# A macaron block on one core: the down product of an FFN chunk stands four chunks behind its gate product instead of three, and its input has five buffers instead of four

## The reference

```python
x = x + 0.5 * ffn(layernorm(x))
x = x + attn(layernorm(x))
x = x + 0.5 * ffn(layernorm(x))
```

```python
scores = sigmoid(x @ gate_w); topk_w, topk_i = top_k(scores, 6)
combine = sum(one_hot(topk_i) * (topk_w / sum(topk_w)))
act = silu(x @ wg) * (x @ wu)                 # all 32 experts
routed = einsum('tef,efd,te->td', act, wd, combine)
shared = silu(x @ sg) * (x @ su) @ sd
```

## Time and profile before

| | |
|---|---|
| median of 3 runs | 1780.58 us (1778.83 to 1783.36) |
| the profiled execution, its own time | 1783.27 us |
| its span, first to last instruction | 1781.4 us |
| mean granted TensorE clock | 0.958 of full speed |
| busy share PE / DVE / POOL / ACT | 87% / 71% / 56% / 47% |

### The profile page before, as it was taken

One profiled execution on the slowest core, in us unless ns is written; L12 is line 12 of the kernel. 1 busy time (PEld: TensorE's weight loads), 2 busy tenths in 40 slices (PEclk: granted clock), 3 DMA queues, 4 the chain that ended last, 5 costly groups with the idle time before them and its releaser, 6 DMA issues. The chain is left out here.

```text
span 1781.4 us, 22496 instructions
## 1 busy us (share of the span) xinstructions
PE 1551.8 (87%) x7088; PEld 1165.3 (65%) x7088; DVE 1265.5 (71%) x2067; ACT 843.5 (47%) x1692; POOL 988.8 (56%) x1048
## 2 busy tenths in 40 slices
PE   5998887887899889888998799879987998889979
PEld 4665554546566567666776677667765776667868
DVE  4553587876868788968797879778977787777321
ACT  4443454543555346535553466346634564444323
POOL 1663354654767457636665566447644666458525
PEclk9999999999999999999999999999998999889989
DMA  4565221123323232423232333233322333233434
GB/s 161 205 217 192 75 95 50 63 77 103 133 90 113 97 121 92 138 88 116 95 126 96 98 115 128 89 104 116 126 95 73 124 114 113 80 112 131 133 100 149
DMA packets 73430, 202.35 MB, mean 114 GB/s; under 512 B 10049, under 2 KB 22561, under 8 KB 72929
## 3 DMA queue, kind: packets, MB, share of 16 engines
q1 hardware_dynamic: 65120, 175.75, 29.6%
q0 software_dynamic: 8192, 25.17, 4.6%
HBM read 175.46 MB, written 25.43 MB: 113 GB/s over the span
## 5 line engine op out<-in xcount | busy, mean ns | idle before, releaser
L1478 POOL TENSOR_TENSOR ring<-ring 128x512 f32<-128x512 f32 x192 | 256.9, 1338 | 378.9 <-DVE ring L1358 378.6
L808 PE MATMUL gub<-x_hi,wr 128*128 128x384 f32 (+2 forms) x1040 | 428.9, 412 | 29.1 <-DVE hid L1175 22.4
L889 PE MATMUL acc<-hid,w_down 128*128 128x384 f32 (+2 forms) x1040 | 408.1, 516 | 15.6 <-POOL hid L1457 15.5
L1457 POOL TENSOR_TENSOR hid<-hid,u_sb 128x384 f32<-128x384 f32 (+2 forms) x260 | 292.0, 1123 | 182.2 <-ACT u_sb L1041 168.0
L810 PE MATMUL gub<-x_hi,wr 128*128 128x384 f32 (+2 forms) x1040 | 370.0, 356 | 0.0
L809 PE MATMUL gub<-x_lo,wr 128*128 128x384 f32 (+2 forms) x1040 | 369.8, 356 | 0.0
L1352 DVE TENSOR_TENSOR_SCAN ring<-decays,side 128x512 f32<-128x512 f32 x256 | 310.4, 1213 | 40.1 <-ACT decays L1139 37.3
L1051 ACT ACTIVATE hid<-gub 128x384 f32<-128x384 f32 (+2 forms) x324 | 156.6, 483 | 365.9 <-PE gub L850 189.5
L1041 ACT ACTIVATE u_sb<-gub 128x384 f32<-128x384 f32 (+2 forms) x260 | 132.2, 508 | 336.6 <-PE gub L810 336.5
L1465 POOL TENSOR_TENSOR hid<-hid,weight 128x384 f32<-128x384 f32 (+2 forms) x240 | 267.6, 1116 | 29.6 <-ACT weight L1031 15.0
L889 PEld LDWEIGHTS acc<-hid,w_down 128*128 128x128 f32 x1040 | 185.7, 192 | 110.9 <-issue 41.8
(11 more groups left out here) (117 smaller groups left out, 1856.8 us busy)
## 6 DMA issues: line engine op xcount, KB each, us to landing
wr<-w_halves SPq DMA_DIRECT2D x234, 512.0 KB, 3.3
wm_gu<-in_w_mlp POOLq DMA_DIRECT2D x64, 256.0 KB, 3.1
w_halves<-wr SPq DMA_DIRECT2D x26, 512.0 KB, 3.2
wm_down<-in_w_mlp POOLq DMA_DIRECT2D x64, 128.0 KB, 2.7
w_raw<-in_w_gu SPq DMA_DIRECT2D x26, 256.0 KB, 3.7
rows<-parts SPq DMA_DIRECT2D x16, 384.0 KB, 2.3
cst<-rows SPq DMA_DIRECT2D x48, 128.0 KB, 2.5
xin<-in_x SPq DMA_DIRECT2D x8, 256.0 KB, 3.0
```

What stands on the lines that cost most here:

```text
L808: mm(out, w[:, 0, half, k, :], x_hi[:, k, a:b], start=(k == 0), stop=False)
L889: last = mm(acc[k][:, a:b], w, h[:, a:b], start=(c == 0), stop=(c == (MLP_CHUNKS if mlp else FFN_CHUNKS) - 1))
L1457: nc.gpsimd.tensor_tensor(h, h, u_sb[c % USLOTS][:, a:b], ALU.mult).then_inc(sem["hidden"], 1)
L1478: add(ysum, ysum, ring[:, ring_at(it)], ALU.add).then_inc(sem["y_sum"], 1)
```

## The change

```diff
-WSLOTS, MSLOTS, HSLOTS, USLOTS = 6, 3, 4, 3
+WSLOTS, MSLOTS, HSLOTS, USLOTS = 6, 3, 5, 3
...
-DLAG = 3
+DLAG = 4
```

## The result

The changed kernel takes 1762.86 us, the median of 9 runs (1759.3 to 1772.78). The kernel before, run beside it, takes 1779.09 us (9 runs, 1775.97 to 1783.67). The ratio is 0.9905, with an interval of [0.9881, 0.9929]: 0.95% faster, 16.9 us of 1779. I had forecast 11.6.

What follows compares the result with a forecast made beforehand. PE was taken as the engine to follow, with 230 us idle to win from. Savings of 2 x 3.4 + 3.1 + 1.65 = 11.55 us, off the median of 1780.58, gave 1769.0 us; range 1761 to 1779.

Steps and rivals of the forecast that it cites:

- steps 3 and 5: POOL's products of chunks 24, 25 pass the sums of units 4, 5 at the ends; 3.4 us saved each.
- step 7: At its end, PE's 3.58 us of waits shrink to about 0.5; 3.1 us saved.
- steps 2, 4, 6: At their ends, DVE's by_g of chunk 25 leaves the stretch after unit 4's L1358; 0.55 us saved each.
- step 1: Wait of 1.6 us at 512 columns; DVE's unit 5 ends almost with the last down, so 0, bound 1.6.
- what is late next: At the ends of steps 3 and 5, rt2 needs unit 5's L1358; 0.3 us of room, 0.2 taken off.
- The norm product beside POOL: Product of chunk 25 falls beside norm product L1247 in steps 3 and 5; 0 added, bound 0.7 us.
- Rival B: Odd steps come to look like even ones, each winning only 0.5 us; about 1777.4 us, 17 in 100.
- rival C: New phase of light items makes gate products wait for banks that by_g frees; about 1790 us, 10 in 100.
- Rival A: Half-clock stretches at ends of steps 3, 5, 7 go too, 5.1 us more; about 1763.9 us, 12 in 100.

Runs made afterwards that it cites:

- pool_swap: Kernel before, with POOL's products of chunks 24 and 25 put ahead of the sums of units 4 and 5 in steps 3, 5 and 7: 0.9906.
- body_only: Kernel before, with downs four chunks behind up to chunk 18, three behind from then on, and five buffers: 0.9991.
- end_only: Kernel before, with downs three chunks behind up to chunk 18, none at chunk 22, four behind from chunk 19 on, and five buffers: 0.9927.
- lag5: Changed kernel with downs five chunks behind instead of four and six buffers instead of five: 1.0012 against the kernel before.

## Why the prediction was right, and where it was off

The forecast was 1769.0 against a median of 1780.58, and faster. It came faster by 16.9 us instead of 11.6, inside the range. The sum was a sum of idle time of PE, 11.55 us, and the idle time fell by 12.9. That the two lie so near each other is in part luck, for the terms missed both ways:

| term | forecast | measured at the ends |
|---|---|---|
| steps 3 and 5 | 2 x 3.4 | 2 x 1.81 |
| step 7 | 3.1 | 3.58 |
| steps 2, 4, 6 | 3 x 0.55 | 1.05, 1.12, 1.12 |
| step 1 | 0, bound 1.6 | 0.08 |
| sum | 11.55 | 10.6 |

The 2.3 us that are left to 12.9 lie in the bodies. (Step 2: `rt2` waited 1.05 us before and not at all after. Steps 4 and 6: 1.58 + 1.48 became 1.60 + 0.34. Step 1: a wait of 1.60 went and one of 1.52 for L1358 came; a longer wait ahead of one of its last C broadcasts, 1.09 for 0.27, is counted with the bodies.)

**The mechanism** was right: the product of chunk 25 stood in POOL's queue behind a sum that waited for DVE. POOL's order alone brings the gain and takes it back.

**Steps 3 and 5: the step "what is late next" was mis-sized.** I gave `rt2` 0.3 us of room, and it lacked 1.48. PE's work from the end of L914 to its end without waits was to be 11.1 us; it is 9.8 (1124.80 to 1136.39 is 11.6, less 0.29 and 1.48). The DVE chain to the end of the L1358 of unit 5 was to be 10.9 and is 11.5 (1124.80 to 1136.29). The delay of ACT's L1066, estimated at 0.95, is 0.98 (1124.80 to 1125.78). So the error is on PE's side for 1.3 us and on DVE's for 0.6. The 11.1 was read off rows that had waits and half clock in them, and I took out only the 3.58. The last down before ran partly at half clock, so `rt2` came 2.13 us behind its start (1149.74 to 1151.87) and comes 1.55 behind it now; PE also stood 0.27 us ahead of L986; and two downs that are held apart took 1.45 + 1.56, while two in a row take 2.75. That makes 1.1 of the 1.3 us.

**The norm product beside POOL** was mis-priced. I put it at 0, with a bound of 0.7, from the means of 1074 and 727 ns. These means mix two kinds, as the shortest, the middle and the longest of the 16 show (kernel before):

```profile
L1247 DVE SCALAR_TENSOR_TENSOR xn_mlp<-hn,lnw,rstd x16: 478/1224/1505, 396.8 to 1675.1; 128x256 f32<-128x256 f32 x16
```

Read one by one, an instruction of L1247 takes 0.48 us, or 0.95 to 1.52 where a sum or a product of POOL had begun before it or with it. L1247 runs 32 times; all 16 long ones of the kernel before and all 17 of the changed kernel end 0.28 us after that POOL instruction ends. (Above: the pair ends at 1131.20 + 2.38 = 1133.58, the product at 1132.13 + 1.18 = 1133.31.) A POOL instruction that begins during one of L1247 is mostly longer too, 1.18 for 0.99. The Trainium skill (SBUF — State Buffer, Who interferes with whom) has the one that issues second wait for the whole of the other's instruction, and the rows here agree. My mean of a third of a microsecond hid it.

So the pair takes 1.90 us when one of the two is held and 2.38 when both are. In steps 3 and 5 the change went from the first to the second, which is 0.48 of DVE's 0.6. In steps 4 and 6 it went from 2.38 to 1.90, and that is most of what these ends won beyond the 0.55 forecast.

**Rival B** (17 in 100) came true in part: the odd steps did come to look like the even ones in their `rt2`, by 1.48 us, under the 2 us that I had set as its mark. It took 3.2 us off the forecast for steps 3 and 5, not 8.4.

**Step 7** was better than forecast: 0.5 us of wait was to stay, none did. Against it stands one new wait in the same step's body:

```profile
1405.82 0.41 PE L808 MATMUL gub<-x_hi,wr 128*128 128x384 f32 x1 [3.96 <-DVE hid L1175]
```

This is rival C's mechanism, and a stretch of half clock follows it (1406.2 to 1409.6), but in one place and not in six, and the total for that row fell.

**Rival A got too little weight.** I had seen the half-clock stretches behind the ends of steps 3, 5 and 7 and priced them at 5.1 us, but gave the case 12 in 100 because PE waits for DVE in the MLP part, "so PE's time would be given back". Of the 5.3 us by which the gain passed my 11.6, the idle time makes 1.3, and 4.0 are rest. In the profiles less work at half clock is worth 4.7 us, and all three stretches behind the ends are at 2.4 GHz; in `pool_swap`, which moves nothing but six POOL instructions, the waits give 8.7 us and the rest 8. So the clock's part was not all given back. The forecast of rival A, 1763.9, is 1 us off the median. But its sign, a rise of the mean granted clock, did not come in the profile (0.958 both times). The Trainium skill (TensorE: Matmul & The Clock Gate, Why this matters for your kernels) advises against idle gaps of some 3 us between bursts of matmuls; here single gaps of 2.9 us with one of 0.7 ahead had a 3.4 us stretch of 1.2 GHz behind them, and gaps of 0.77, or of 0.29 and 1.48, had none.

How firm that is: the same gaps of 0.7 and 2.87 us stand at three ends of `body_only`, and only the one of step 5 has half clock behind it:

```profile
775.30:778.70 3.40, 3.40 (x16) 2.60 (x17) 1.77 (x7) 0.00 (x0) 0.00 (x0) 1.00 0.03 5
1142.20:1145.60 3.40, 3.40 (x11) 2.52 (x10) 2.57 (x8) 0.00 (x0) 0.00 (x0) 0.50 0.19 70
1512.70:1516.10 3.40, 3.40 (x15) 2.49 (x16) 1.79 (x7) 0.00 (x0) 0.00 (x0) 1.00 0.08 26
```

Elsewhere shorter gaps have it: in the kernel before, a gap of 1.81 us that ends at 1309.59, with no other in the 8 us ahead of it, is followed by 3.4 us at 0.50 from 1310.8 on. Nor is the size of the clock's part steady from kernel to kernel. As rest it is -8 us in `pool_swap`, -4 in the changed kernel and about 0 in `end_only` (idle -13.1, ratio 13.0), with intervals of 4 to 6 us to either side, so these three are not told apart; it is +8 in `lag5`. A run's own mean clock goes from 0.950 to 0.958 over the nine runs of the changed kernel, and its time by some 13 us. So which gaps bring a half-clock stretch, and whether the new phase of the body brings more of them, stays open.

## What to carry to other kernels

Read the end of a pipeline once for each engine's queue. The gain here was not the longer distance of the down, which no chunk in the body needed, but that two elementwise products passed two sums that were waiting for someone else, and the same gain was to be had by moving those alone in one queue.

Where a wait of about 3 us in a busy PE is taken away, look at the granted clock just behind it and count that stretch too, as a term with its own chance. Then look at the clock of the whole span as well: a stretch that is gone in one place can stand in another.

A mean over instructions that sometimes run beside another engine is no price for one that does. Look at the shortest and the longest, and at what ran beside them.

A longer distance needs one buffer more, or it turns into a wait on the side of the producer (here 2.5%), and going one further (five) lost all the gain, through longer waits and more half clock in places that the ends do not show.

## What the runs showed of the hardware that I had not expected

- Half-clock stretches behind short waits: PE was 87% busy over the run, and yet waits of 2.86 us, with 0.72 a little ahead of them, were followed by 3.4 us at 0.50 to 0.51 of full clock. With waits of 0.77 us there the clock stayed at 1.00. In `body_only` two of three such places kept full clock with waits of 0.7 and 2.87, so the wait alone does not decide it.
- The mean granted clock differs between runs of one and the same kernel, 0.950 to 0.958 over nine, and the slowest run had the lowest clock: 1772.78 us at 0.950, 1759.3 at 0.958.
- An instruction of the norm product, with two SBUF inputs, takes 0.48 us on DVE. Beside a POOL sum or product that had begun before it or with it, it took 0.95 to 1.52 and ended 0.28 us after that one, in all 33 cases of the two profiles.
